# Attention probabilities turned by DMA transposes from a row layout instead of by TensorE, with the value matmuls six tiles behind

## What is computed

```python
x = L0_attn_hidden_states                      # [1, 1024, 512] f32
xn = _layernorm(x, axis=-1)
x = x + _L0_attn_ref(xn, ...) + _L0_ffn_ref(xn, ...)

# in _L0_attn_ref: H = 32 heads, NOPE = 128, ROPE = 64, VD = 128, Q_RANK = 192, KV_RANK = 64
q_lat = rmsnorm(hidden_states @ q_a_w, q_a_norm_w)
q = (q_lat @ q_b_w)                            # per head: q_nope (128), q_pe (64), q_pe rotated
kv = (rmsnorm(kv_lat, kv_a_norm_w) @ kv_b_w)   # per head: k_nope, v
scores = (q_nope . k_nope + q_pe . k_pe) * QKD ** (-0.5)
mask = topk_mask & causal                      # 128 keys per row, by the indexer's scores
attn = softmax(where(mask, scores, -inf))
out = einsum('bhqk,bhkd->bqhd', attn, v).reshape(b, s, H * VD)
return out @ o_w
```

## Time and profile before

| | |
|---|---|
| runs | 1023.12, 1024.95, 1027.54 us; median 1024.95 |
| the profiled execution | span 1021.7 us, 25695 instructions; its time outside the profile isn't stated |
| busy, share of the span | TensorE 88%, VectorE 73%, ScalarE 67%, GpSimd 44% |
| queue q1 (DMAs), share of the 16 DMA engines | 15.2%, 51.31 MB |
| attention stage | about 370 to 929 us |

### The profile page before, as it was taken

One profiled execution on the slowest core, in us unless ns is written; L12 is line 12 of the kernel. 1 busy time (PEld: TensorE's weight loads), 2 busy tenths in 40 slices (PEclk: granted clock), 3 DMA queues, 4 the chain that ended last, 5 costly groups with the idle time before them and its releaser, 6 DMA issues.

```text
span 1021.7 us, 25695 instructions
## 1 busy us (share of the span) xinstructions
PE 896.0 (88%) x7912; PEld 548.5 (54%) x7912; DVE 741.3 (73%) x1593; ACT 680.6 (67%) x1512; POOL 450.1 (44%) x307
## 2 busy tenths in 40 slices
PE   5979999966764789998989989989989989989998
PEld 2434554434420266666666656656666656665443
DVE  5385699999999877876787777767767868783000
ACT  3656689977853488786777778768868868873000
POOL 2193239876548454363354436426335525600000
PEclk9999999997777899999999999999999999999999
DMA  7011111113344800000000000000000000220211
GB/s 223 22 36 57 52 48 57 41 36 99 100 147 157 305 23 22 2 23 23 22 3 23 22 3 22 22 3 22 22 8 17 22 23 2 90 98 22 62 41 41
DMA packets 47259, 52.67 MB, mean 52 GB/s; under 512 B 5440, under 2 KB 31424, under 8 KB 47168
## 3 DMA queue, kind: packets, MB, share of 16 engines
q1 hardware_dynamic: 47168, 51.31, 15.2%
HBM read 36.62 MB, written 6.29 MB: 42 GB/s over the span
## 4 chain that ended last, share of the span: by engine, by line
PE 50%; issue 18%; POOL 14%; DVE 11%; ACT 3%; DMA 1%; DVEq 1%; SPq 0%; ACTq 0%; POOLq 0%
PE psS L575 11%; PE psS L684 8%; PE psT L652 8%; PE psO L633 6%; POOL arena L1409 4%; PE psT L450 4%; DVE m L1103 3%; POOL arena L1411 3%; PE psS L474 3%; ACT arena L714 2%; PE psS L427 2%; POOL arena L1420 2%; POOL arena L1418 2%; DVE bias L1107 1%; PE psT L560 1%
## 5 line engine op out<-in xcount | busy, mean ns | idle before, releaser
L714 ACT ACTIVATE arena<-psT 128x512 f16<-128x512 f32 (+5 forms) x544 | 263.4, 519 | 145.5 <-PE psT L652 101.5
L968 DVE SCALAR_TENSOR_TENSOR arena<-psT,arena 128x512 f16<-128x512 f32 (+3 forms) x392 | 205.9, 553 | 89.1 <-ACT arena L714 89.1
L575 PE MATMUL psS<-keyT,arena 128*128 128x512 f16 (+3 forms) x1152 | 231.7, 329 | 13.8 <-POOL arena L1420 12.3
L1202 DVE CUSTOM_DVE_ANT_0 arena<-psS,bias 128x1024 f32<-128x1024 f32 (+7 forms) x256 | 192.6, 752 | 50.2 <-PE psS L575 48.0
L914 ACT ACTIVATE arena<-arena,small 128x1024 f32<-128x1024 f32 (+7 forms) x256 | 199.2, 778 | 18.4 <-DVE small L1202 15.8
L652 PE MATMUL psT<-ident,arena 128*128 128x128 f32 x1152 | 177.7, 281 | 26.8 <-issue 17.7
L633 PEld LDWEIGHTS psO<-val,arena 128*128 128x128 f16 x3456 | 132.6, 98 | 38.7 <-DVE arena L968 6.0
L575 PEld LDWEIGHTS psS<-keyT,arena 128*128 128x128 f16 x1152 | 104.2, 99 | 86.1 <-issue 34.1
L633 PE MATMUL psO<-val,arena 128*128 128x64 f16 x3456 | 143.9, 193 | 1.5 <-DVE arena L968 1.2
L652 PEld LDWEIGHTS psT<-ident,arena 128*128 128x128 f32 x1152 | 123.6, 141 | 32.0 <-issue 23.7
L1401 POOL TENSOR_TENSOR arena<-arena,cq 128x1024 f32<-128x1024 f32 x16 | 37.8, 2364 | 214.8 <-ACT arena L714 214.8
(11 more groups left out here) (146 smaller groups left out, 1111.4 us busy)
## 6 DMA issues: line engine op xcount, KB each, us to landing
arena<-in_wiq SPq DMA_DIRECT2D x32, 256.0 KB, 2.7
arena<-in_ow SPq DMA_DIRECT2D x16, 512.0 KB, 4.8
arena<-arena SPq DMA_DIRECT2D x32, 256.0 KB, 2.3
arena<-in_qbT SPq DMA_DIRECT2D x16, 256.0 KB, 2.5
wvo_parts<-arena SPq DMA_DIRECT2D x16, 256.0 KB, 4.6
arena<-in_qpe SPq DMA_DIRECT2D x16, 128.0 KB, 2.6
arena<-in_x SPq DMA_DIRECT2D x8, 256.0 KB, 2.7
out<-arena SPq DMA_DIRECT2D x8, 256.0 KB, 2.0
```

The source lines that it names most:

```text
L575: last = mm(psS[k % 2][:, c:c + w], Q[:, v, a, h, t * P:(t + 1) * P], keyT[:, b, h, c:c + w], start=(a, b) == (0, 0), stop=(a, b) == (1, 0))
L714: return nc.scalar.activation(dst, src, ACT.Copy, scale=scale)
L968: return v.scalar_tensor_tensor(out=dst, in0=src, scalar=scale, in1=hi, op0=ALU.mult, op1=ALU.subtract)
L1202: v.tensor_tensor_reduce(out=pr[:, k % 4, 0:kw], in0=psS[k % 2][:, 0:kw], in1=bias[:, TOFF[t]:TOFF[t + 1]], scale=-c_s, scalar=3e38, op0=A ...
```

## The change

- TensorE no longer turns the probabilities. ScalarE copies a whole row of `pr` to f16 (`hi_step`), VectorE makes its low part (`low_step`), side by side in a buffer `pp`, both still with the queries on the partitions. SP then issues one transposing DMA for the tile (`turn`): it turns all 2 x `NB[k]` blocks of 128x128 f16 of `pp` into `pT`.
- There are four slots (`s % 4`) of `pr`, `pp` and `pT`, each as long as its longest row. A `turn` waits for the row's low part and for the value matmuls of four tiles before; a `hi_step` waits for the transpose of four tiles before.
- The scores have four banks (`psS[0]`, `psT[0]`, `psS[1]`, `psT[1]`) and are no longer written three tiles ahead: a step of TensorE is the scores of tile `s` and the value matmuls of tile `s - 6` (`LAG`).
- The query jobs and `out_T` share the one bank left, `psT[2]`, and stand at other steps: `Q_AT` 0, 1, 3, 5 (before 0, 2, 5, 9), `O_AT` 8, 10 (before 4, 8).
- VectorE's `head_out` comes six tiles after the head's end. SP's `swap` of the next pair stands ahead of the pair's 16 transposes, and the loads of the output weights ahead of the last pair's.
- The arena grows from 15040 to 17152 words per partition; the space set aside for DMA descriptors by the program (`dynamic_dma_scratch_size`) is made 2048.

```diff
...
-ARENA = 15040
+ARENA = 17152
...
-        pr = view(7168, 4 * S).rearrange("p (u k) -> p u k", u=4)
-        pT = view(11264, 4 * S, F16).rearrange("p (u s k) -> p u s k", u=2, s=2)
-        op = view(13312, NT * P).rearrange("p (k r) -> p k r", k=NT)
-        lat32 = view(13312 + NT * P, CH)
+
+
+        SLOT = [P * max(NB[k] for k in range(j, NT, 4)) for j in range(4)]
+        SLOT_AT = [sum(SLOT[:j]) for j in range(5)]
+        pr = [view(7168 + SLOT_AT[j], SLOT[j]) for j in range(4)]
+        PP_AT = 7168 + SLOT_AT[4]
+        pp = [view(PP_AT + SLOT_AT[j], 2 * SLOT[j], F16) for j in range(4)]
+        PT_AT = PP_AT + SLOT_AT[4]
+        pT = [view(PT_AT + SLOT_AT[j], 2 * SLOT[j], F16).rearrange("p (b q) -> p b q", q=P) for j in range(4)]
+        OP_AT = PT_AT + SLOT_AT[4]
+        op = view(OP_AT, NT * P).rearrange("p (k r) -> p k r", k=NT)
+        lat32 = view(OP_AT + NT * P, CH)
...
+        s_bank = [psS[0], psT[0], psS[1], psT[1]]
...
-        AHEAD = 3
+        LAG = 6
         ROPE_AT = 8
-        Q_AT, O_AT = {0: 0, 2: 1, 5: 2, 9: 3}, {4: 0, 8: 1}
-        RING = []
-        for s_ in range(16):
-            RING += [("T", s_, c) for c in range(NCH[s_ % 8])]
-            RING += [("Q", Q_AT[s_])] if s_ in Q_AT else []
-            RING += [("O", O_AT[s_])] if s_ in O_AT else []
-        RING_AT = {use: n for n, use in enumerate(RING)}
-        USES = len(RING)
-        assert USES % 3 == 0
+        Q_AT, O_AT = {0: 0, 1: 1, 3: 2, 5: 3}, {8: 0, 10: 1}
+
+        def turned_by(p, s):
+            return 16 * (4 * p + s // 4 + 1)
...
-            with sp.Fori(1, NP) as p:
-                swap(p)
+            def turn(p, s, first):
+
+                j, kw = s % 4, P * NB[s % 8]
+                wait_alone(sp, p_lo, 16 * p + s + 1)
+                if not (first and s < 4):
+                    wait_alone(sp, av_mm, 16 * p + s - 3)
+                sp.dma_start_transpose(pT[j][:, 0:2 * NB[s % 8], :], pp[j][:, 0:2 * kw]).then_inc(turned[j], 16)
+
+            def turns(p, first):
+                for s in range(16):
+                    turn(p, s, first)
+
+            swap(1)
+            turns(0, True)
+            with sp.Fori(1, NP - 1) as p:
+                swap(p + 1)
+                turns(p, False)
...
+            turns(NP - 1, False)
...
-                    pe.wait_ge(max_done, 16 * p + s - 1)
+                    pe.wait_ge(max_done, 16 * p + s - 3)
                 for a, b in ((0, 0), (0, 1), (1, 0)):
                     for c in range(0, kw, CH):
                         w = min(CH, kw - c)
-                        last = mm(psS[k % 2][:, c:c + w], Q[:, v, a, h, t * P:(t + 1) * P], keyT[:, b, h, c:c + w],
+                        last = mm(s_bank[k % 4][:, c:c + w], Q[:, v, a, h, t * P:(t + 1) * P], keyT[:, b, h, c:c + w],
...
+            def values(p, s):
+
+                k, head = s % 8, 2 * p + s // 8
+                pe.wait_ge(turned[k % 4], turned_by(p, s))
                 if k == 0 and not (isinstance(head, int) and head == 0):
                     pe.wait_ge(o_done, head)
                 dst = psO[:, k * KVR:(k + 1) * KVR]
                 for j in range(NB[k]):
                     for n, (a, b) in enumerate(((0, 0), (0, 1), (1, 0))):
-                        last = mm(dst, pT[:, k % 2, a, j * P:(j + 1) * P], val[:, b, j, :],
+                        last = mm(dst, pT[k % 4][:, a * NB[k] + j, :], val[:, b, j, :],
                                   start=j == 0 and n == 0, stop=j == NB[k] - 1 and n == 2)
                 last.then_inc(av_mm, 1)
...
             def pair(p, v, first, last_pair):
                 for s in range(16):
-                    k = s % 8
-                    pe.wait_ge(exp_done, 16 * p + s + 1)
-                    for c in range(NCH[k]):
-                        n = RING_AT[("T", s, c)]
-                        wait_bank(p, n, first, last_pair)
-                        for j in range(4 * c, min(4 * c + 4, NB[k])):
-                            last = nc.tensor.transpose(psT[n % 3][:, (j % 4) * P:(j % 4 + 1) * P],
-                                                       pr[:, k % 4, j * P:(j + 1) * P], ident[:])
-                        last.then_inc(t_mm, 1)
                     if s in Q_AT and not last_pair:
-                        n = RING_AT[("Q", Q_AT[s])]
-                        wait_bank(p, n, first, last_pair)
-                        q_job(psT[n % 3][:], p + 1, Q_AT[s])
+                        j = Q_AT[s]
+                        if j == 0 and not first:
+                            pe.wait_ge(ot_lo, 2 * p - 2)
+                        elif j == 1 or j == 2:
+                            pe.wait_ge(raw_done, 2 * p + j + 2)
+                        elif j == 3:
+                            pe.wait_ge(qa_hi, 6 * p + 9)
+                        q_job(psT[2][:], p + 1, j)
                     if s in O_AT and not first:
-                        n = RING_AT[("O", O_AT[s])]
-                        wait_bank(p, n, first, last_pair)
-                        out_T(psT[n % 3], p - 1, O_AT[s])
-                    if s + AHEAD < 16:
-                        scores(p, v, s + AHEAD, False)
-                    elif not last_pair:
-                        scores(p + 1, 1 - v, s + AHEAD - 16, False)
-                    if s:
-                        values(2 * p + (s - 1) // 8, (s - 1) % 8)
+                        c = O_AT[s]
+                        if c:
+                            pe.wait_ge(ot_lo, 2 * p - 1)
+                        elif not last_pair:
+                            pe.wait_ge(qa_hi, 6 * p + 12)
+                        else:
+                            pe.wait_ge(ot_lo, 2 * p - 2)
+                        out_T(psT[2], p - 1, c)
+                    if not (first and s == 0):
+                        scores(p, v, s, first and s < 4)
+                    if s >= LAG:
+                        values(p, s - LAG)
                     elif not first:
-                        values(2 * p - 1, 7)
-
-            scores(0, 0, 2, False)
+                        values(p - 1, s - LAG + 16)
+
+            pe.wait_ge(vo_hi, 2 * NP)
             pair(0, 0, True, False)
             with pe.Fori(0, NP // 2 - 1) as i:
                 pair(2 * i + 1, 1, False, False)
                 pair(2 * i + 2, 0, False, False)
             pair(NP - 1, 1, False, True)
-            values(H - 1, 7)
+            for s in range(16 - LAG, 16):
+                values(NP - 1, s)
...
+            def hi_step(p, s, fresh):
+
+                j, kw = s % 4, P * NB[s % 8]
+                act.wait_ge(exp_done, 16 * p + s + 1)
+                if not fresh:
+                    act.wait_ge(turned[j], turned_by(p, s - 4))
+                copy(pp[j][:, 0:kw], pr[j][:, 0:kw], PR_S).then_inc(p_hi, 1)
...
             def pair(p, v, first, last_pair):
+                for s in range(16):
+                    if s in Q_AT and not last_pair:
+                        q_evac(psT[2][:], p + 1, 1 - v, Q_AT[s])
+                    if s in O_AT and not first:
+                        ot_evac(psT[2], p - 1, O_AT[s])
+                    exp_step(p, s)
+                    if s:
+                        hi_step(p, s - 1, first and s <= 4)
+                    elif not first:
+                        hi_step(p - 1, 15, False)
...
+                    wait_alone(dve, p_lo, 16 * p + s - 3)
...
+            def low_step(p, s):
+                j, kw = s % 4, P * NB[s % 8]
+                dve.wait_ge(p_hi, 16 * p + s + 1)
+                low(pp[j][:, kw:2 * kw], pr[j][:, 0:kw], PR_S, pp[j][:, 0:kw]).then_inc(p_lo, 1)
...
             def pair(p, v_, first, last_pair):
+                for s in range(16):
+                    if s == LAG and not first:
+                        head_inv(p - 1, 1)
+                        head_out(p - 1, 1)
+                    if s == LAG + 8:
+                        head_inv(p, 0)
+                        head_out(p, 0)
+                    row_max(p, s, first and s < 4)
+                    if s >= 2:
+                        low_step(p, s - 2)
+                    elif not first:
+                        low_step(p - 1, s + 14)
+                    if s in O_AT and not first:
+                        ot_low(psT[2], p - 1, O_AT[s])
+                    if s == ROPE_AT and not last_pair:
+                        rope_hi(p + 1, 1 - v_)
```

95 lines of the change are left out of this document (10 added, 85 removed).

## The result

The changed kernel takes 1133.94 us (median of four runs, 1131.8 to 1135.44); the kernel before, run beside it, took 1026.24 us (1023.12 to 1028.05). The ratio is 1.106, 95% interval 1.103 to 1.109. The sign of the forecast was right and its size wrong: +108 us where +22 stood, and outside the range of 1000 to 1112. The profiled execution has a span of 1130.0 us.

The account below looks back on a forecast made before the run. TensorE was taken as the bound, 96% busy in an undisturbed pair. 37.5 us a pair against 36.57 gave +14 over fifteen pairs; with +1, +4 and +3 that made +22 and 1047 us, range 1000 to 1112.

Parts of the forecast that it names:

- What is moved on ScalarE and VectorE: Attention pairs: whole rows read from SBUF replace PSUM pieces; 0.5 us saved, ScalarE 27.6 and VectorE 27.0 us a pair.
- The source gives nothing: Claim that reading SBUF instead of PSUM changes no duration: VectorE's low part 683 ns from PSUM, 693 from SBUF.
- What is removed: 72 TensorE transposes a pair, 8.1 us, leaving about 25.6 us of TensorE work; worth up to 122 us if unhindered.
- The query jobs: Next pair's query jobs stand closer together: chain 12.0 us against 7.6 of ScalarE work, swap 1.5 us late.
- the stand: ScalarE's idle once a pair before its copy to `lat32`, waiting for GpSimd's low parts: up to 4.4 us.
- The DMA: 144 transposed blocks a pair at about 0.12 us, 17 us, hidden; SP issue 0.5 to 0.6 us each.
- One pair: Sum along the query chain and VectorE's following work, with 1.0 us for other waits: 37.5 us against 36.57.
- The ends: Outside the repeating pairs: first pair +1 us, output-weight loads ahead of last transposes +4, last transposing DMA +3.
- Rival 3: TensorE's clock falls to 0.8 in the attention stage: about +1 us a pair, 1062 us; chance 0.12.
- Rival 2: The transposing DMAs bound the pair: at 0.29 us a block 43 us a pair, 1129 us; chance 0.20.
- Rival 1: ScalarE's stand is absorbed; ScalarE and VectorE bind the pair at 34 us, 994 us; chance 0.20.
- signs named: ScalarE idle 2 to 5 us a pair, swap wait over 0.75, DMAs under 20; wrong if clock under 0.9.

Follow-up runs that it names:

- e8: Changed kernel with GpSimd's seven instructions a pair cut to 64 columns from the third pair on: 1020.71 us, ratio 0.995.
- e4: Kernel before, with VectorE's low part reading its first source from SBUF instead of PSUM, plus one self-wait: 1149.05 us, ratio 1.122.
- e7: Kernel before with only the extra VectorE self-wait of e4, low part's source left in PSUM: 1025.51 us, ratio 1.001.
- e3: Changed kernel with the edits of e1 and e2 together: 995.88 us, ratio 0.973.
- e1: Changed kernel with a second buffer for query jobs, so ScalarE no longer waits for the previous job's low parts: 1127.82 us, ratio 1.100.
- e2: Changed kernel with exponentials written into the scores' PSUM bank, so VectorE's low part has one PSUM source: 1091.77 us, ratio 1.064.
- e5: Changed kernel with an ordinary SBUF-to-SBUF copy of the same bytes in place of each transposing DMA: 1114.38 us, ratio 1.085.
- e9: e3 with ordinary copies in place of the transposing DMAs: 984.83 us, ratio 0.960.

## Why the prediction was wrong, step by step

**What is moved on ScalarE and VectorE: the step that failed.** "The source gives nothing", by 683 against 693 ns. The 693 ns is that of an instruction at 36.4 us, with no GpSimd instruction beside it, and it is right: e8 has 700. But a duration of an instruction alone does not tell what it is beside another engine's. VectorE's 27.0 us a pair became 318.57 / 400 x 42.1 = 33.5, longer by about what the exclusion adds (6.7), and it became the busiest engine, 80% of a longer pair. The case had two tests at hand: GpSimd works 16.5 us a pair, all of it from SBUF, and no VectorE instruction of the stage before had two sources in SBUF. Had the prediction asked of each moved operand who else reads that memory, it would have asked the right question; the Trainium skill's page "SBUF — State Buffer", named above, answers it. e4, e7 and e8 show it from three sides.

**What is removed** was right: at the full clock, in e3's loop, TensorE works 255.80 / 320 x 32.4 = 25.9 us a pair, where 25.6 was forecast; in the changed kernel 65.6 us of its busy time are gone in spite of a lower clock. Given nothing else in the way it is worth what e3 shows, 36.5 - 32.6 = 3.9 us a pair, not 8.1, since ScalarE and VectorE take over as busiest (84% and 82% in e3's stretch).

**The query jobs**: the mechanism was right and its size nearly, 5.4 us at the copy to `lat32` against "up to 4.4", the swap late by 2.1 us against 1.5. (With the rows' own factors and the 0.1 us off for each of the 13 instructions, ScalarE's work in between is 7.2 us and not 7.6, and the stand up to 4.8.) Its weight was not: 6 us of time beside the exclusion (e1), 96 without it (e2 against e3).

**The DMA.** Inside its bounds of 0.083 and 0.29 us a block but 0.175 and not 0.12; 25.2 us a pair, not 17. It was called hidden and costs 1.1 us a pair in the changed kernel (e5) and none in e3 (e9). SP's part was off as well: from 500 to 900 us a transposing DMA took 1.43 us to issue (median of 153, 1.17 to 2.09), not 0.5 to 0.6, which is 23 us a pair on SP; the ordinary copies of e5 took 0.47. SP still didn't hold the pair: e3 has the same issues in 32.4 us. The Trainium skill, page "DMA: Bandwidth & Descriptors", section "Latency and other measured facts", gives the 261 GB/s for one kernel with a non-contiguous middle dimension and 350 to 400 for the contiguous case; the trace is below both, 32 KB in 0.175 us being 187 GB/s. If each block took 1309 ns, a pair would have taken over four times as long as it did. So the Trainium skill's figure on the page "VectorE: DVE Perf Modes", section "The three transpose paths", is not the price of a block in a stream of them.

**One pair.** 37.5 forecast, 42.1 found. Even with the exclusion out and the stand in it is 39.5 (e2), where scores also wait for the low part, so about 2 us of waits between the engines were missing from the sum beside the 1.0 allowed. Part of the gap is a slip: by the earlier trace rows a low part costs 0.133 us a block and 0.151 (284 less 133 ns) for the start, not 0.09; the twelve come to 9.0 us and not 8.3, and the forecast pair to 38.2, which would have made about 1058 us.

**The ends.** Against the +1 for the first pair stand the 5.0 us before the second product with `sq`, but they are no loss of the start: the first of these products starts at 365.48 and before at 367.41 (its job stands one tile earlier now), and the next comes 41.5 us later against 34.6. From the start of the last score matmul (1027.4) to the first product (1036.93) 9.5 us, before 5.1: +4.4 against +3. The loads ahead of the last pair's transposes: a stand of 14.3 us against +4, because no slot hides a transfer that is queued behind 4 MB. Of the 29.7 us behind the thirteen pairs, 5.6 are one more pair, 14.3 and 4.4 these two; 5.4 were not followed up.

**The rivals.** Rival 3 came true beside the rest: the clock of the stage is 0.85 with TensorE at 70% and standing for up to 4.3 us at a time. No run separates its cost. Rival 2 did not decide. Rival 1, with its 34 us a pair and 994, was the state of e3 (32.6 and 996), not of this change. Of the signs named, the stand and the later swap came; a clock under 0.9 and DMAs over 20 us a pair said that the forecast was off. The cause that decided was none of the three rivals.

## What to carry to other kernels

Moving a tensor from PSUM to SBUF can cost nothing on the instruction alone and 12% of a kernel beside GpSimd: before such a move list every VectorE instruction that will then have two inputs in SBUF, and put GpSimd's busy time in the same stage next to it. When a change opens two obstacles at once, take each away alone and both together: one alone was worth 6 us here, the other 42, and both 138. Look in a profile for means that don't grow with the number of columns; they are waits that the trace books as busy time.

## What was not expected of the hardware

The exclusion shows as busy time on both sides and in no list of waits: 88.5 us on VectorE and 28.5 on GpSimd. A transposing DMA of f16 from SBUF to SBUF, two to sixteen blocks each and following one another, took twice an ordinary copy of the same bytes (0.175 against 0.088 us per 128x128 block). And the granted clock did not follow TensorE's busy share alone. In the loop, from 500 to 820 us, e8, e4 and e2:

```profile
500.00:820.00 320.00, 254.22 (x3003) 150.72 (x3004) 251.46 (x525) 261.33 (x549) 41.72 (x84) 0.95 0.79 155
```

```profile
500.00:820.00 320.00, 261.15 (x2793) 174.44 (x2790) 270.29 (x462) 207.40 (x478) 128.72 (x68) 0.94 0.04 15
```

```profile
500.00:820.00 320.00, 237.95 (x2574) 141.56 (x2572) 217.96 (x458) 222.58 (x471) 135.32 (x74) 0.89 0.68 133
```

TensorE is 80% busy at a clock of 1.00 in e3, 79% at 0.95 in e8, 82% at 0.94 in e4 and 74% at 0.89 in e2. Its longest single wait in the same stretch is 1.8 us in e3, 2.5 in e8, 3.0 in e4 and 3.4 in e2, and 4.3 in the changed kernel at 0.85. The kernel before has one of 3.1 us at 0.99, with TensorE 93% busy. That long waits are the cause was not tried.
